# Spreading the up half's evictions and eight quarter experts of the weight fold over twelve gate steps of a quantized feed-forward

## The reference, cut to what matters

```python
def act_qdq(x):
    qmax = 2.0 ** (ACT_BITS - 1) - 1.0
    scale = jnp.maximum(jnp.max(jnp.abs(x)) / qmax, 1e-12)
    return jnp.clip(jnp.round(x / scale), -qmax - 1.0, qmax) * scale
...
x = act_qdq(x)
up = act_qdq(x @ lpbq_dequant(w_up).T)
gate = act_qdq(x @ lpbq_dequant(w_gate).T)
sig = fixed_qdq_u16(jax.nn.sigmoid(gate))
gate = act_qdq(gate * sig)
o = act_qdq(gate * up)
return o @ lpbq_dequant(w_down).T
```

## Time and profile before

| | |
|---|---|
| device time, median of 3 runs | 1929.24 us (1924.55 to 1931.20) |
| the profiled execution, its device time | 1929.26 us |
| the profiled execution, its span | 1927.6 us |
| PE busy, share of the span | 91% |
| DVE busy | 49% |
| ACT busy | 19% |

### The profile page before, as it was taken

How to read it: one execution, slowest core, us unless ns; L and a number is a source line. 1 busy time by engine, 2 the same in 40 slices (tenths; PEclk the granted TensorE clock), 3 DMA queues, 4 the chain that set the end, 5 groups by cost and what they waited for, 6 DMA issues and landing times. The chain is left out here.

```text
span 1927.6 us, 32039 instructions
## 1 busy us (share of the span) xinstructions
PE 1757.1 (91%) x13350; PEld 1097.1 (57%) x13350; DVE 943.0 (49%) x2520; ACT 374.6 (19%) x635; POOL 305.4 (16%) x150
## 2 busy tenths in 40 slices
PE   5879789999999999778799998999999976998998
PEld 2347678887888888764344443444444455447443
DVE  1326888768687785407311111111114497236676
ACT  2222111120111201001011111111113639133200
POOL 0000413151331514200394000000000000004000
PEclk9988899999999999789899999999999988999999
DMA  7000000000000000025310001200001044000000
GB/s 305 33 0 6 2 2 8 2 9 8 2 8 2 9 7 3 8 79 232 150 47 1 0 0 73 123 0 0 0 0 55 0 155 139 6 0 1 6 17 22
DMA packets 20043, 73.33 MB, mean 38 GB/s; under 512 B 3530, under 2 KB 8130, under 8 KB 17090
## 3 DMA queue, kind: packets, MB, share of 16 engines
q1 hardware_dynamic: 19906, 71.37, 9.9%
HBM read 69.26 MB, written 2.10 MB: 37 GB/s over the span
## 5 line engine op out<-in xcount | busy, mean ns | idle before, releaser
L563 POOL TENSOR_TENSOR peer_bm<-peer_bm,peer_slots 128x512 f32<-128x512 f32 x64 | 193.9, 3029 | 609.1 <-DVE peer_bm L650 609.1
L436 PE MATMUL peer_ps_h<-all_x,layer_down 128*128 128x256 f32 (+1 forms) x1024 | 241.3, 390 | 0.4 <-issue 0.4
L474 PE MATMUL peer_ps_o<-peer_hg,layer_up 128*128 128x256 f32 x1024 | 226.6, 382 | 1.5 <-DVE peer_hg L682 1.5
L474 PEld LDWEIGHTS peer_ps_o<-peer_hg,layer_up 128*128 128x128 f32 x1024 | 195.9, 192 | 33.3 <-issue 5.2
L436 PEld LDWEIGHTS peer_ps_h<-all_x,layer_down 128*128 128x128 f32 x1024 | 192.9, 193 | 28.4 <-issue 2.5
L1129 DVE SCALAR_TENSOR_TENSOR skills_hid<-skills_ps_u,all_pair_w,skills_act_g 128x512 f32<-128x512 f32 x64 | 48.0, 751 | 294.7 <-PE skills_ps_u L1091 294.7
L451 PE MATMUL peer_ps_w<-peer_bm,peer_am 64*64 64x32 f32 x8192 | 144.5, 227 | 31.9 <-DVE peer_hg L682 25.1
L451 PEld LDWEIGHTS peer_ps_w<-peer_bm,peer_am 64*64 64x64 f32 x8192 | 137.1, 144 | 52.1 <-issue 52.1
L508 ACT ACTIVATE peer_hg<-peer_ps_h 128x512 f32<-128x512 f32 x128 | 76.4, 597 | 371.7 <-PE peer_ps_h L436 371.7
L652 DVE TENSOR_TENSOR peer_am<-all_iota_a,peer_slots 128x2048 f32<-128x2048 f32 x64 | 146.2, 2285 | 0.0
L1108 ACT ACTIVATE skills_act_g<-skills_ps_g 128x512 f32<-128x512 f32 x96 | 57.3, 597 | 438.0 <-PE skills_ps_g L1091 438.0
(11 more groups left out here) (288 smaller groups left out, 2228.0 us busy)
## 6 DMA issues: line engine op xcount, KB each, us to landing
quant_w<-in_l_w SPq DMA_DIRECT2D x64, 256.0 KB, 4.3
lora_w<-in_l_w SPq DMA_DIRECT2D x8, 1024.0 KB, 8.7
four_skill<-in_skills SPq DMA_DIRECT2D x2, 3072.0 KB, 12.9
skills_w<-in_skills SPq DMA_DIRECT2D x2, 3072.0 KB, 15.1
skills_w<-in_skill_shared SPq DMA_DIRECT2D x2, 3072.0 KB, 22.0
layer_down<-in_down SPq DMA_DIRECT2D x1, 4096.0 KB, 24.3
layer_up<-in_up SPq DMA_DIRECT2D x1, 4096.0 KB, 33.5
swiglu_w<-in_cond SPq DMA_DIRECT2D x2, 1541.0 KB, 8.2
```

What stands on the lines that cost most here:

```text
L436: mm = pe.matmul(ps_h[group % 2][:, r, :], down[:, c, j * P:(j + 1) * P], g.x[:, c, bass.ds(i * PB, PB)], start=(c == 0), stop=(c == C - 1))
L474: mm = pe.matmul(ps_o[:, c, :], up[:, j, c * P:(c + 1) * P], hg[half][:, j, :], start=(j == 0), stop=(j == NJ - 1))
L563: pool.tensor_tensor(bm[c % RING][:], bm[c % RING][:], slots[half][:, 2, c * PAIRS:(c + 1) * PAIRS].unsqueeze(2).to_broadcast([P, PAIRS, WJ]),
```

## The change

Four edits, all in `quant_ffn`:

- PE: the up projections come two per gate step, and after two of every three steps one quarter expert is folded, eight in all (experts 0 and 1). The other 24 quarters follow the last projection.
- ACT: two evictions of the up half in each of the 12 gate steps (before: four in each of the first six), one on either side of the next step's rounding. Experts 0 and 1 are evicted after the gate phase, four of them in the product phase and two in the down phase (before: one, six and one). In the product phase the gated step is rounded ahead of the up step.
- DVE: one up maximum in every gate step from the second on, and the last behind the last gate maximum. The scale of the gated part (3) is now formed ahead of that of the up part (2).
- POOL: the five reductions run in the order 0, 1, 3, 2, 4, and the waits for them follow it.

```diff
+        order = (0, 1, 3, 2, 4)
...
-                dve.wait_ge(spread, n + 1)
+                dve.wait_ge(spread, order.index(n) + 1)
...
                 peak(part(gate, i), peaks[:, 1, i:i + 1])
-                if 5 <= i < 11:
-                    for k in range(2 * (i - 5), 2 * (i - 5) + 2):
-                        dve.wait_ge(kept, n_up + 2 * k + 2)
-                        peak(part(up, k), peaks[:, 2, k:k + 1])
-                if i == 10:
-                    gather(2, peaks[:, 2, :])
+                if i > 0:
+                    dve.wait_ge(kept, n_up + 2 * i)
+                    peak(part(up, i - 1), peaks[:, 2, i - 1:i])
             gather(3, peaks[:, 1, :])
+            dve.wait_ge(kept, n_up + 2 * len(STEPS))
+            peak(part(up, len(STEPS) - 1), peaks[:, 2, len(STEPS) - 1:len(STEPS)])
+            gather(2, peaks[:, 2, :])
+            scales(3, scale[:, 1:2])
             scales(2, scale[:, 0:1])
-            scales(3, scale[:, 1:2])
...
-            for n in range(5):
+            for n in order:
                 pool.wait_ge(vstep, marks["top", n])
...
-            for q in range(NBLK):
-                for m in range(MQ):
-                    project(n_up + q * MQ + m, 0, q, m)
-            for n in range(4 * E3):
-                e, i = divmod(n, 4)
...
+            for i in range(len(STEPS)):
+                for k in range(2 * i, 2 * i + 2):
+                    project(n_up + k, 0, k // MQ, k % MQ)
+                if i % 3 != 2:
+                    fold(i - i // 3)
+            for n in range(8, 4 * E3):
+                fold(n)
             pe.wait_ge(kept, n_down)
...
             for i in range(len(STEPS)):
-                for k in range(4 * i, 4 * i + 2):
-                    if i < 6:
-                        keep_part(n_up, up, k)
+                keep_part(n_up, up, 2 * i)
                 if i + 1 < len(STEPS):
                     round_gate(i + 1, 1)
-                for k in range(4 * i + 2, 4 * i + 4):
-                    if i < 6:
-                        keep_part(n_up, up, k)
+                keep_part(n_up, up, 2 * i + 1)
                 sigmoid(i)
             keep_fold(0)
+            keep_fold(1)
             for i in range(len(STEPS)):
+                round_gate(i, 3)
                 round_up(i)
-                round_gate(i, 3)
-                if i in (0, 1, 3, 5, 8, 10):
-                    keep_fold((0, 1, 3, 5, 8, 10).index(i) + 1)
+                if i in (2, 5, 7, 10):
+                    keep_fold((2, 5, 7, 10).index(i) + 2)
             for i in range(len(STEPS)):
                 round_gate(i, 4)
-                if i == 2:
-                    keep_fold(E3 - 1)
+                if i in (2, 6):
+                    keep_fold((2, 6).index(i) + 6)
```

More of the change, by code:

```diff
@@ L1328, in project, with fold @@
                 mm.then_inc(mm_ready, 1)
+            def fold(n):
+                e, i = divmod(n, 4)
+                pe.wait_ge(loads[n % NSLOT], 32 * (n // NSLOT + 1))
+                if i == 0 and e >= 3:
+                    pe.wait_ge(w_kept, e - 2)
+                for f in range(2):
+                    for c in range(C):
+                        mm = pe.matmul(ps_w[e % 3][:, c, :], w1[n % NSLOT][:, f, c * P:(c + 1) * P], w2[n % NSLOT][:, f, :],
+                                       start=(i == 0 and f == 0 and c == 0), stop=(i == 3 and f == 1), skip_group_check=True)
+                mm.then_inc(folded, 1)
             for n, r in enumerate(first_rounds):
```

## The result

The changed kernel takes 1913.98 us (median of 5 runs, 1911.93 to 1914.16) against 1929.24 us (1924.55 to 1931.20). The ratio is 0.9922 with a 95% interval of 0.9907 to 0.9937, so it is faster by 0.8%. The forecast was 1911.4 us with a range of 1907.0 to 1915.5: right in direction and size, the measured median 2.6 us above it. The profiled execution has a span of 1912.4 us, 15.2 less than before.

The account below looks back on a forecast made before the run. The gate phase was taken as bound by PE, then DVE. ACT starting the product phase 17.3 us sooner plus 0.6 us within it gave 17.9 off 1929.26: 1911.4 us, range 1907 to 1915.5, folds and down phase adding nothing.

Parts of the forecast that it names:

- Bound: Gate phase runs first behind PE, steps 6.87 us apart, then behind DVE, steps 5.97 us apart with two up maxima each.
- Rival (c): Gate phase: DVE's 5.97 us steps have another cause than the second maximum, so 1928.7 us; chance 0.03.
- Gate phase: DVE paces gate steps at 4.85 us, PE close behind at 4.61; ACT begins the product phase 17.3 us sooner.
- Product phase: From ACT's product start to the gather: two evictions fewer save 1.0 us, a wait costs 0.35, so 0.6 us gained.
- Folds: Quarter experts on PE end about 1603 us, bank waits 0.4 us at most, off the path; costed at nothing.
- Down phase: Slow PE clock after idling costs the same 2.1 us as before, uncertain by -2.1 to +2.1 us.
- The sum: Whole kernel: 1929.26 us minus 17.9 gives 1911.4 us, 0.93% less; forecast as it stands has chance 0.80.
- (a): Gate phase: PE takes over as the limit, giving 1913.7 us, or 1914.3 with DVE's rounding waits; chance 0.14.
- the 1.65 us of cover: End of the gate phase: PE's last projection is ready 1.65 us early, all the cover the eight quarters have.
- (b): PE's clock falls while alternating projections and folds; with half the work slow, 1946 us, slower than before; chance 0.03.

Follow-up runs that it names:

- The experiment with the old order: Changed kernel with the old order of scales, POOL reductions and product-phase roundings (up first): median 1917.49 us, ratio to before 0.9909.
- the constant on ACT: Changed kernel with all projections ahead of the quarter experts, and ACT instead of DVE removing the gate phase's rounding constant: 1908.64 us, ratio to before 0.9875.

## Why the prediction was right

**Bound.** That the gate phase ran behind PE and then behind DVE is confirmed by undoing each half: with the old evictions the steps are again 6.87 us long, with the old maxima 5.97 us, and 4.14 us come back. Rival (c), that the 5.97 us have another cause than the second maximum, falls with this: a step with one maximum takes 4.84 us in the same program.

**Gate phase.** Each step of the sum, with the 1.5 us taken off: first sigmoid 1511.6 (forecast 1511.5); third step 1521.6 (1521.6); step 4.84 (4.85); last step 1564.6 (1564.65); last projection done at 1561.1 (1561.2); second gather 1570.25 (1570.36); product phase 1571.2 (1571.3). The gain was 17.45 us by the marks, 17.3 forecast.

**Product phase.** 0.67 us shorter from its start to its gather (0.6 forecast), made of one microsecond for two evictions of experts and a return of 0.3: the waits for ACT that the forecast placed behind an expert's eviction stand in steps 3 and 11, 0.27 and 0.26 us. The experiment with the old order gave 0.29 us for it.

**Folds.** Done at 1603.6 (1603 forecast), one wait of 0.79 us where at most 0.4 was worked out, off the path as said. What the prediction did not say, and the runs show, is that these eight quarters need not have moved at all.

**Down phase.** This is the term that was mis-sized, inside the ±2.1 us it was given: I took the same loss as before, 2.1 us, and it was 2.85. Before had the smallest loss of all kernels without a fill (2.1 against 2.5 to 3.0), so its trace alone led low. That the range held this is no merit of the sum: the term was known from one execution only. The Trainium skill's statement in "TensorE: Matmul & The Clock Gate" ("What's actually happening") that the slow start differs between runs of a kernel is borne out by 0.2 us between the two executions of the changed kernel, and by the head of the stage, which is the same in all kernels: there one execution of thirteen lost 2.1 us more than the others.

**The sum.** From the first instruction of the stage to the first down matmul the gain was 18.12 us (17.9 forecast). With 0.78 less in the down phase it is 17.34. The span has 1.52 us more ahead of the stage and 0.62 behind it, 15.2 in all. Both lie in parts that are the same in all kernels, where the table's rows differ by 11 us ahead of the stage and by 1.7 us behind it, so neither needs a cause in the change. The prediction let the runs of before speak for this only in its lower end; it should have stood in the upper one too.

**Rivals.** (a) did not come, by the 1.65 us of cover, and came with 3.5 us as soon as the cover was used up. (b) did not come: PE changed between projections and folds with no idle time and its clock was 1.00 from 1506 to 1571 and 0.98 in the next 41 us, in which the idling ahead of the down phase begins (1.00 in its first 32 us, up to 1603). The rule of the Trainium skill ("TensorE: Matmul & The Clock Gate", "A second HAM failure mode: psum-queue depth-cycling") speaks of small idle times between groups, and this kernel has none; going through banks alone does not bring the clock down here. Two of the experiments come nearer to it: without the quarters PE waits 0.34 and 1.14 us for banks among the projections, and with the constant on ACT five times 0.32 to 0.47 us, and the clock stays at 1.00 there too.

## What to carry to other kernels

When two engines are each fully busy in one half of a phase and half idle in the other, the tie between them is an order that someone wrote down: find the instruction that couples their paces (here four evictions per gate step) and spread it so that both run at the pace of the slower one, then sum each engine's pieces per step to see how much cover is left. Undo each part of such a change on its own, since a part that sounds right (the quarters among the projections) may be worth nothing. Where PE idles ahead of a phase that it bounds, a few matmuls into a free bank just before it took the slow start off the path here; leave as little idling as possible between them and the phase.

## What the runs showed of the hardware

- After PE had idled 11.4 to 14.1 us the down phase began with 4 to 6 us of matmuls at 1.2 GHz; the loss was 2.1 to 3.0 us over eight executions of seven kernels, and no less after 6.54 us of idling (2.6 us, the kernel with the constant on ACT).
- After 2.80 us of idling the clock fell once PE was back at work, at a cost of 1.7 us; after 1.09, 0.97 and 0.51 us it did not. Each was seen in one execution.
- Three unused float32 matmuls of 128x512, 4.99 us and most of it at half clock, brought the clock back as well as fourteen that bridged the idling, in one execution of each.
- Waits of 0.32 to 1.14 us between groups of projections, in two kernels, left the clock at 1.00.
- The part of the program ahead of the stage, the same in every kernel, ended between 1454.5 and 1465.9 us. What varies in it was not looked into.
